# A sandwich of attention and FFN: input loads put behind a block's exit, score and value stages no longer interleaved, and the transposes before the FFN moved into the loop that makes their rows

## The reference

```
Z   = layernorm(x)
X   = Z[:, :256, :];  Y = Z[:, 256:, :]
U   = B_l X;  W = C_l X                      # 256 x 256 weights
att = relu(U^T W);  att[2047, 2047] = 0      # 2048 x 2048 per batch
X'  = X + A_l (X att);  Y' = Y + r_l (Y att)
x1  = x + layernorm(concat(X', Y'))
h   = silu(layernorm(x1) gate_w^T * gate_s) * (layernorm(x1) up_w^T * up_s)
out = x1 + layernorm(h down_w^T * down_s)    # inner width 5632
```

## Time and profile before

| | us |
|---|---|
| median of three runs | 1398.87 |
| the profiled execution, its own time | 1398.94 |
| its span on the slowest core (core 0) | 1397.2 |
| span of the other cores | 1393.5 to 1396.2 |
| first matmul of ub | 35.2 |
| first score matmul | 78.4 |
| first value chain | 120.1 |
| end of the last value chain | 321.2 |
| first instruction of the x1 loop | 328.3 |
| last copy to lnfT ends | 408.5 |
| first FFN matmul | 413.7 |
| last block begins | 1342.4 |

### The profile page before, as it was taken

One profiled execution on the slowest core, in us unless ns is written; L12 is line 12 of the kernel. 1 busy time (PEld: TensorE's weight loads), 2 busy tenths in 40 slices (PEclk: granted clock), 3 DMA queues, 4 the chain that ended last, 5 costly groups with the idle time before them and its releaser, 6 DMA issues. The chain is left out here.

```text
span 1397.2 us, 13089 instructions; the slowest of 8 cores (1393.5 to 1397.2 us)
## 1 busy us (share of the span) xinstructions
PE 1142.4 (82%) x5236; PEld 505.3 (36%) x5236; DVE 372.0 (27%) x481; ACT 235.8 (17%) x309; POOL 46.8 (3%) x68
## 2 busy tenths in 40 slices
PE   0366788991069999999999999999999999999930
PEld 0012233340034444444444444444444444444410
DVE  2008543435630102210132011311023101230385
ACT  0234131436541000000000000000000000000045
POOL 2000000000010000000000000000000000000000
PEclk9779799996559999999999999999999999999975
DMA  9910000002389432283514754066530863303048
GB/s 258 197 21 1 0 1 0 1 0 91 150 150 167 75 66 55 33 148 66 93 24 63 120 93 87 0 96 117 89 61 0 129 112 61 61 0 61 0 160 321
DMA packets 28748, 112.86 MB, mean 81 GB/s; under 512 B 2448, under 2 KB 5008, under 8 KB 24208
## 3 DMA queue, kind: packets, MB, share of 16 engines
q0 software_dynamic: 22784, 75.24, 32.3%
q1 hardware_dynamic: 5040, 35.69, 7.2%
q10 hardware_dynamic: 864, 1.10, 0.3%
HBM read 170.48 MB, written 16.78 MB: 134 GB/s over the span
## 5 line engine op out<-in xcount | busy, mean ns | idle before, releaser
L768 PE MATMUL ps_f<-lnfT,gw_sb 128*128 128x512 bf16 x1408 | 312.8, 380 | 5.8 <-PEq L74 5.8
L820 PE MATMUL ps_f<-dwb,hdn 128*128 128x512 bf16 x1408 | 304.9, 379 | 11.4 <-DVE hdn L798 11.4
L784 PE MATMUL ps_f<-lnfT,uw_sb 128*128 128x512 bf16 x1408 | 311.1, 379 | 0.0
L798 DVE SCALAR_TENSOR_TENSOR hdn<-ps_f,us_sb,sg 128x1024 bf16<-128x1024 f32 x44 | 56.5, 1284 | 555.2 <-PE ps_f L784 555.2
L820 PEld LDWEIGHTS ps_f<-dwb,hdn 128*128 128x128 bf16 x1408 | 137.3, 98 | 178.9 <-issue 14.1
L768 PEld LDWEIGHTS ps_f<-lnfT,gw_sb 128*128 128x128 bf16 x1408 | 138.1, 98 | 173.2 <-issue 8.3
L784 PEld LDWEIGHTS ps_f<-lnfT,uw_sb 128*128 128x128 bf16 x1408 | 137.8, 98 | 166.1
L794 ACT ACTIVATE sg<-ps_f,gs_sb 128x1024 bf16<-128x1024 f32 x44 | 49.0, 1114 | 831.3 <-PE ps_f L768 831.3
L833 DVE TENSOR_TENSOR acc<-acc,ps_f 128x2048 f32<-128x2048 f32 x40 | 91.5, 2287 | 172.1 <-PE ps_f L820 172.1
L486 PE MATMUL ps_t<-att,xTb 128*128 128x512 bf16 x512 | 114.0, 385 | 18.4 <-DVE attn_out L514 18.4
L486 PEld LDWEIGHTS ps_t<-att,xTb 128*128 128x128 bf16 x512 | 50.6, 99 | 81.2 <-issue 22.5
(11 more groups left out here) (104 smaller groups left out, 405.1 us busy)
## 6 DMA issues: line engine op xcount, KB each, us to landing
gw_sb<-gw POOLq DMA_DIRECT2D x22, 1024.0 KB, 9.5
uw_sb<-uw POOLq DMA_DIRECT2D x22, 1024.0 KB, 9.9
dwb<-dw POOLq DMA_DIRECT2D x11, 2048.0 KB, 20.2
xbuf<-x SPq DMA_DIRECT2D x8, 1024.0 KB, 27.9
x1sp<-xbuf SPq DMA_DIRECT2D x8, 1024.0 KB, 3.8
x1rb<-x1sp SPq DMA_DIRECT2D x8, 1024.0 KB, 15.7
y<-acc SPq DMA_DIRECT2D x8, 1024.0 KB, 8.0
xTb<-xT POOLq DMA_DIRECT2D x4, 1024.0 KB, 62.6
```

Source lines behind the costliest of these rows:

```text
L768: e.matmul(ps_f[:, half, :], gw_sb[:, slot, ht * P:(ht + 1) * P], lnfT[:, ht, half * 512:(half + 1) * 512], start=(ht == 0), stop=(ht == H ...
L784: e.matmul(ps_f[:, 2 + half, :], uw_sb[:, slot, ht * P:(ht + 1) * P], lnfT[:, ht, half * 512:(half + 1) * 512], start=(ht == 0), stop=(ht ...
L798: pl.vop(lambda e, gi=gi, li=li: e.scalar_tensor_tensor(hdn[:, li, :], ps_f[:, 2:4, :], us_sb[:, gi:gi + 1], sg[:, gi % 2, :], ALU.mult, A ...
L820: e.matmul(ps_f[:, bs + hc, :], hdn[:, li, tt * P:(tt + 1) * P], dwb[:, li, hc * 512:(hc + 1) * 512], start=(li == 0), stop=(li == blk - 1)),
```

## The change

- **Loads.** The identity goes first on SP, and xtop is issued by ScalarE's queue. The loads of x (SP) and of xTb (POOL) move from block 0 to the start of block 1. One counter serves all of x, so that each tile's statistics wait for all 8 tiles.
- **Statistics of x.** They stand first in VectorE's list of block 1; the coefficients are made once for all tiles, behind the column sums of q = 0.
- **Order in a quarter.** Everything of a quarter now stands together: 16 score tiles, column sums, t0(2), broadcast, t0(3), tx(0), t0(4), tx(1), t0(5), mix, t0(6), t0(7), t0(0), t0(1). Relus alternate between ScalarE and VectorE from q = 1.
- **Before the FFN.** Block 2 is gone. The second half of each turn of the x1 loop now makes that tile's statistics (5 small VectorE instructions, Ln and Exp on ScalarE, 2 more on VectorE), casts the tile into the space of xTb, transposes it, and copies the four groups to lnfT_v (the space of att2), groups 0 and 2 by ScalarE, 1 and 3 by VectorE.
- **FFN.** The first four weight loads now stand at the start of the FFN's block, ahead of those of dwb.
- **Last block.** w1f is bf16 where it was float32.

```diff
 # block 0
+    pl.dma("sXI", "sync", ident_sb[:, :], t_ident.ap())
     for jt in range(JT):
-        pl.dma("sXT", "sync", xtop_sb[:, jt, :],
+        pl.dma("sXT", "scalar", xtop_sb[:, jt, :],
...
-    for dt in [2, 3, 4, 5]:
-        pl.dma("sXI", "sync", xbuf[:, dt, :], t_x.ap()[dt * P:(dt + 1) * P, :])
...
-    for k in range(4):
-        pl.dma("sXTB", "gpsimd", xTb[:, 4 * k:4 * k + 4, :],
...
 # block 1
+    for dt in range(DT):
+        pl.dma("sXI", "sync", xbuf[:, dt, :],
+               t_x.ap()[dt * P:(dt + 1) * P, :])
+    XI = pl.v("sXI")
+    for k in range(4):
+        pl.dma("sXTB", "gpsimd", xTb[:, 4 * k:4 * k + 4, :],
...
+    for dt in range(DT):
+        ln_stats(xbuf[:, dt, :], muvar1[:, dt, :], w_extra=[("sXI", XI)])
...
+        t0_chain(2)
...
+        t0_chain(3)
         pl.vop(lambda e: e.tensor_copy(colsumB[:, :], ps_sh[:, 1, :]),
...
+        csb_done = pl.v("sDV")
+        epilogue(2)
+        tx_chain(0)
+        t0_chain(4)
+        epilogue(3)
+        tx_chain(1)
+        txb_done = pl.v("sDV")
+        t0_chain(5)
+        epilogue(4)
...
 # in the x1 loop, for each dt, behind the store of x1
+        pl.aop(lambda e, dt=dt: e.activation(
+            lnt[:, dt:dt + 1], t2c[:, :], AF.Ln, bias=c_eps),
+            w=[("sDV", vst)])
+        pl.aop(lambda e, dt=dt: e.activation(
+            rF[:, dt:dt + 1], lnt[:, dt:dt + 1], AF.Exp, scale=c_nh))
...
+        wcast = [("sDV", ngfd), ("sPE", tr_done.get(dt - 2, t0_last[3]))]
+        pl.aop(lambda e, dt=dt, sl2=sl2: e.activation(
+            xTb_v[:, sl2 * D:(sl2 + 1) * D], xbuf[:, dt, :], AF.Identity,
+            scale=rF[:, dt:dt + 1], bias=ngF8[:, dt:dt + 1]), w=wcast)
...
+            if g4 % 2 == 0:
+                pl.aop(lambda e, dt=dt, g4=g4, pb=pb: e.copy(
+                    lnfT_v[:, g4 * 4:g4 * 4 + 4, dt * P:(dt + 1) * P],
...
+            else:
+                pl.vop(lambda e, dt=dt, g4=g4, pb=pb: e.tensor_copy(
...
 # start of the FFN's block
     pl.new_block()
     load_chunk(0)
     load_chunk(1)
```

More of the change, by code:

```diff
@@ L364, in emit_x1_chain @@
         sq_done[(qp, dt)] = pl.v("sAC")
[L366 to L373, removed]
+    for q in range(NQ):
         qb = q % 2
@@ L411, in sc_stage @@
                 w=[relu_cnt[(q, NT - 1)], relu_cnt[(q, NT - 2)], ("sSM", SM)])
[L412 to L436, removed]
+            att_fix = pl.v("sDV")
         w0 = [relu_cnt[(q, NT - 1)], relu_cnt[(q, NT - 2)]]
+        if att_fix:
+            w0.append(("sDV", att_fix))
         if 0 in sh_free:
@@ L449, in mid_stage, with t0_chain @@
                w=[("sPE", cs_mm)])
-        cs_ev[q] = pl.v("sAC")
-        wb1 = [("sAC", cs_ev[q])]
+        cs_ev = pl.v("sAC")
+        if q == 0:
+            emit_r1_coeffs()
+        t0_mm_val = {}
+        def t0_chain(dt):
+            bidx = dt % 3
+            wt0 = [("sXTB", XTB)]
+            if bidx in pst_free:
+                wt0.append(("sDV", pst_free[bidx]))
+            for nt in range(NT):
+                pl.em("tensor",
+                      lambda e, dt=dt, nt=nt, qb=qb, bidx=bidx:
+                      e.matmul(ps_t[:, bidx, :],
+                               xTb[:, nt, dt * P:(dt + 1) * P],
+                               att2[:, qb, nt, :],
+                               start=(nt == 0), stop=(nt == NT - 1)),
+                      w=(wt0 if nt == 0 else ()),
+                      inc=("sPE" if nt == NT - 1 else None))
+            t0_mm_val[dt] = pl.v("sPE")
@@ L471, in mid_stage @@
                                txb[:, jt, :], start=(jt == 0), stop=(jt == 1)),
-                      w=([("sDV", txb_done[q]), ("sWB0", WB0)]
+                      w=([("sDV", txb_done), ("sWB0", WB0)]
                          if jt == 0 else ()),
                       inc=("sPE" if jt == 1 else None))
[L475 to L524, removed]
-                tmpn[:, 0:MQ], attn_out[:, dt, qsp], AF.Square,
-                accum_out=sqacc[:, dt, qp:qp + 1]),
-                w=[("sDV", epi_done[(qp, dt)])])
-            sq_done[(qp, dt)] = pl.v("sAC")
-        if q == NQ - 1:
-            emit_x1_chain(dt)
@@ L553, in build_nc @@
+        t0_chain(6)
+        epilogue(5)
+        t0_chain(7)
+        epilogue(6)
+        t0_chain(0)
+        epilogue(7)
+        t0_chain(1)
+        t0_last[q] = t0_mm_val[1]
+        epilogue(0)
+        epilogue(1)
+    psA.close()
+    psT = ExitStack()
+    ps_tr = [psT.enter_context(nc.psum_tensor(f"ps_tr{i}", [P, 4 * P], BF16))
+             for i in range(2)]
+    xTb_v = xTb[:, :, :].rearrange("p a b -> p (a b)")
+    tr_done = {}
+    ev_done = {}
     pl.vop(lambda e: e.reduce_sum(muN8[:, :], nacc[:, :, :],
```

319 lines of the change are left out of this document (161 added, 158 removed).

## The result

The changed kernel takes 1421.75 us (median of 10 runs, the lowest 1420.70), where the kernel before takes 1398.80 (10 runs): 1.0162 times as long, 95% interval 1.0151 to 1.0173. The profiled execution took 1420.88 us with a span of 1419.2 on core 5, so the trace stands for the median within 0.1%.

A forecast was written before the change was run, and what follows sets the result against it. TensorE was taken to wait at four places before the FFN: for amixb, a block's exit, VectorE, and ScalarE and VectorE taking turns. 1398.9 - 27.7 (front) + 38.4 (x1 loop) + 9.4 (FFN's start) = 1419.0 us; range 1403 to 1435.

The forecast's parts named there:

- Block 0 and its exit: Start of kernel: exit waits for POOL's loads; with x and xTb gone, block 1 starts at 39.6 us, not 78.
- rival 3: Block exits wait for all loads, not only POOL's; another cause that stays would give 1447 us; chance 0.03.
- The loads: Start of block 1: x and xTb start together at 39.6 us; x lands at 81, xTb at 96.
- rival 1: Block 1's loads: even engine shares, x lands with xTb, at 94 us; total 1432; chance 0.14.
- Quarter 0: Block 1: TensorE waits for xTb until 96 us, tx(1) waits to 112.7, quarter 0 ends at 134.4.
- the stall's 18.4: Block 1, t0(0): TensorE waits 18.4 us behind VectorE, which reached the statistics of x only at 108.0.
- Turns: Quarters 1 to 3: score matmul to score matmul takes 52.96 us, not 54.98; last value chain ends at 293.5.
- The x1 loop: Before the FFN: tiles serialise at 14.4 and 15.15 us, loop ends at 419.2; 38.4 us lost, the largest term.
- Rival 2: x1 loop overlaps its tiles after all, 6.4 us a tile; kernel takes 1360 us; chance 0.08, with cases between.
- Rival 4: x1 loop: Ln, Exp and the copy need different tables, 20.5 us more, total 1439; chance 0.03.
- The FFN's start: Last copy to first FFN matmul: 14.6 us against 5.2, 9.4 more, with dsB's load adding 3.0.
- The sum: Whole kernel: 1398.9 - 27.7 + 38.4 + 9.4 = 1419.0 us, 1.4% slower.

The follow-up runs named there:

- the order alone: Kernel before with statistics of x first, coefficients at once, new quarter order and relu split; loads and tail stay old: 1371.29 us, 0.9804.
- the loads alone: Kernel before with the loads of x, the identity and xTb moved to the start of block 1, old order kept: 1360.08 us, 0.972.
- both together: Changed kernel up to the last value chain, kernel before from there on, with xtop loaded by SP: 1372.83 us, 0.9812.

## Why the prediction was right, point by point

- **Block 0 and its exit: right.** ub and wb start at 24.9 (25.4 foretold) and block 1 at 39.3 (39.6). That the exit waits for POOL's loads rested on two landings; two experiments now show it, 30.7 to 4.3 us and 5.8 to 1.1. So the case that rival 3 priced at 1447, another cause that stays, is wrong. Its first half stays open: whether an exit also waits for SP's loads was not tried.
- **The loads: right.** x landed at 80.3 (81) and xTb at 92.8 (96): 1.09 times the sum of the two queues' costs, not 1.15. Of the two shares that I weighed, x has the larger one, that of row-long packets (65.6% of the engines, 7.4 KB a packet against 2.0, as shown above); rival 1, in which x lands at 94 and the time is 1432, is wrong: it took the mean packet of the whole run for that of these two loads. The Trainium skill (DMA: Bandwidth & Descriptors, "Queues, rings and completion order") has the engines change queues at the end of a packet; the landing at 80.3 agrees with that rule and packets as long as a row, and so do the packets from 41 to 79 us, 1136 of one queue and 966 of the other, if the page's packet is the profile's.
- **Quarter 0: right.** The wait for xTb is 35.2 us (38 foretold), tx(1) starts at 112.4 (112.7), quarter 0 ends at 134.2 (134.4). xTb came 3.2 us early, and nothing came of it, since tx(1) waits for the statistics of x. The first chain, behind that wait, costs 2.5 more than the next (6.16 against 3.63 for 16 matmuls), where I had 1.7.
- **Turns: right.** 52.8 and 53.1 (52.96); the last chain ends at 293.4 (293.5).
- **The x1 loop: right in mechanism and size, with a step short.** Up to its start it took 8.4, not 7.1. The last two epilogues, where ScalarE and VectorE take turns, take 4.36 us each (attn_out's L452 at 293.00 and 297.36), more than the 3.45 of a chain. The last L452 begins 4.0 us behind the end of the last chain (297.36 against 293.35), and 2.5 behind it before (L514 at 323.70 against 321.18). Why they lag more was not tested. Tiles take 14.1 to 14.5 and 14.8 to 15.1 us (14.4 and 15.15), the ScalarE copy 0.585 (0.6). The loop ends at 418.9 (419.2). Rival 2, in which tiles overlap, is wrong for this kernel, but its mechanism is real: with another order of the same instructions a tile takes 10.8 to 12.2 us (11.9 over the whole loop, 305.1 to 400.0) and the kernel is as long as before; I had put that point at 12.3. The rival's own price, 6.4 us a tile and a kernel of 1360, left out that ScalarE alone is busy for 8.1 us a tile in that run. Rival 4 is wrong: the loop loads no table.
- **The FFN's start: right, with compensating parts.** 14.5 us from the last copy (14.6). dsB's part is 2.0 and not 3.0; without it, the landing that counts, that on the four cores where it comes later, takes 11.1 to 11.5 and not 10.7. The Trainium skill (DMA: Bandwidth & Descriptors, "Anatomy of one DMA — SWDGE (gpsimd) path") would have 4.4 us for this transfer, an estimate by the 1 MB that it writes (6.8 by the 2 MB of float32 that it reads); even with dsB out of the way it took 8.1 from issue to first matmul at the least, so the measurement decides against it for a load that converts.
- **Not foretold: 2.3 us in the FFN.** From the first FFN matmul to the span's end the eight cores took 982.5 to 983.7 before and 982.2 to 987.1 now. On five of the eight (982.2 to 983.3) there is thus no loss, and on cores 0, 4 and 5 it took 985.7 to 987.1. Windows of the slowest core, its second row starting 3.6 us after the first FFN matmul:

```profile
core 5: us, PE busy (x) PEld busy (x) DVE busy (x) ACT busy (x) POOL busy (x), PEclk, DMA share, GB/s
433.40:437.00 3.60, 3.60 (x9) 1.32 (x10) 0.00 (x0) 0.00 (x0) 0.00 (x0) 0.50 1.00 167
437.00:460.00 23.00, 23.00 (x102) 10.18 (x101) 1.28 (x1) 3.51 (x3) 0.70 (x1) 0.95 1.04 174
```

 And the same stretches of the kernel before:

```profile
413.70:417.30 3.60, 3.59 (x9) 1.29 (x10) 0.00 (x0) 0.00 (x0) 1.50 (x2) 0.51 0.33 109
417.30:440.30 23.00, 23.00 (x108) 10.43 (x107) 1.28 (x1) 3.51 (x3) 0.70 (x1) 1.00 1.02 176
```

 In the 23 us this core made 102 matmuls against 108, at a granted clock of 0.95 against 1.00. At 23.00 / 108 = 0.21 us each that is 1.3 us. The rest is open.

- **The sum: right.** 1419.0 foretold for the profiled execution, 1420.9 measured. Front -27.7 (-27.8), tail to the last copy +38.4 (+38.2, the 1.3 ahead of the loop among them), FFN's start +9.4 (+9.3). That single terms come this close is in part luck: the loop was 1.5 us shorter than foretold (117.1 against 118.6) and the step ahead of it 1.3 longer; in the FFN's start dsB cost 1.0 less and the load alone took up to 0.8 more; xTb came 3.2 early without effect; and the 2.3 in the FFN were not foretold at all.

What the prediction didn't see is where the front's gain comes from. It read as the exit's 30.7 us and the stall's 18.4, less the wait for xTb. The runs show two changes that each do without the other: the order alone wins 28 us, the loads alone 39, both together only 26. The new order lets the exit's gain run into the wait for xTb, and takes away sc(1), which had stood ready to fill it.

## What to carry to other kernels

Before a load is moved behind a barrier, look at what the consumer's queue has to do until it lands: here the same move was worth 39 us with independent scores ahead of the consumer, and nothing without. A loop that makes its row tiles to the end, statistics, cast and transposes included, has the whole chain of waits in every turn; put the second half of a turn beside the first half of the next, and weigh it against the split into a loop for the rows and a block for the transposes, which was faster still here. Before a block's exit, leave no transfer in POOL's queue that isn't needed at once.

## What the runs showed of the hardware that I had not expected

Loads land in two groups of four cores, an early and a late one, in all eight kernels in which TensorE waits for xTb. In the changed kernel cores 1, 2, 5 and 7 are the late ones. From xTb's issue to the first value chain it is 51.7 to 52.5 us on the other four and 53.3 to 54.4 on these. From gw_sb's issue to the first FFN matmul it is 9.6 to 11.3 us on four and 13.1 to 13.8 on the late four, and with dsB's load later 8.1 to 8.7 and 11.1 to 11.5. dsB, on ScalarE's queue, lands in 4.8 to 5.2 and 6.5 to 6.8 us.

The groups aren't the dies: 1 and 2 belong to one die, 5 and 7 to the other. Nor are they fixed: with two counters for x the late ones are 0, 3, 4 and 7. But in all eight kernels the late four are one core of each of the pairs 0 and 1, 2 and 3, 4 and 5, 6 and 7, which by chance would come out 16 times in 70 in each. So the two cores of a pair seem to compete for something; no run here has only one core of a pair at work, so the cause is not shown. The slowest core sets the time, so this costs it up to 3 us on a wait for gw_sb and about 2 on one for xTb.
